# GpSimd keeps the gathers and the shuffles: the Wlin sum on VectorE, the value copy on ScalarE, gathers three to a step

## The reference

```python
embed_x = emb_table[X + offsets]             # [2048, 39, 64], a gather of rows of 256 bytes
att = embed_x
for i in range(3):                           # three layers, 2 heads of 32
    q, k, v = att @ WQ[i], att @ WK[i], att @ WV[i]
    attn = softmax(einsum('bihd,bjhd->bhij', q, k))
    att = relu(einsum('bhij,bjhd->bihd', attn, v) + att @ WR[i])
att_output = relu(att.reshape(B, 39 * 64) @ Wlin)
h = relu(embed_x.reshape(B, 39 * 64) @ W1 + b1)   # 512 wide
h = relu(h @ W2 + b2)                              # 256 wide
return sigmoid(att_output + relu(h @ W3 + b3))
```

## Time and profile before

| | before |
|---|---|
| median of three runs | 2331.08 us (2326.01 to 2338.38) |
| the profiled execution | 2338.26 us, span 2336.0 us, so 2.3 us lie around the span |
| TensorE | 2074.0 us busy, 89% of the span |
| VectorE | 1783.2 us, 76% |
| ScalarE | 1225.8 us, 52% |
| GpSimd | 1263.2 us, 54% |
| granted TensorE clock | 0.946 of full speed on the mean |

### The profile page before, as it was taken

One profiled execution on the slowest core, in us unless ns is written; L12 is line 12 of the kernel. 1 busy time (PEld: TensorE's weight loads), 2 busy tenths in 40 slices (PEclk: granted clock), 3 DMA queues, 4 the chain that ended last, 5 costly groups with the idle time before them and its releaser, 6 DMA issues. The chain is left out here.

```text
span 2336.0 us, 105692 instructions
## 1 busy us (share of the span) xinstructions
PE 2074.0 (89%) x44640; PEld 1687.1 (72%) x44640; DVE 1783.2 (76%) x3943; ACT 1225.8 (52%) x3397; POOL 1263.2 (54%) x1838
## 2 busy tenths in 40 slices
PE   1798998988989899898989989989898998989998
PEld 0577776867767777676777767778687776767887
DVE  2677786867868787786787868778687787878997
ACT  0455554645645455564555545556464555545665
POOL 6445555555555655556455555655656555565503
PEclk9999999989999999998999989999999999999998
DMA  4110011101101011010110101011010110101000
GB/s 137 26 26 24 24 28 24 28 22 24 28 23 28 23 28 25 23 29 21 27 26 25 28 22 28 23 25 29 22 30 23 27 25 24 29 21 27 23 20 15
DMA packets 67580, 64.76 MB, mean 28 GB/s; under 512 B 23768, under 2 KB 54504, under 8 KB 67112
## 3 DMA queue, kind: packets, MB, share of 16 engines
q1 hardware_dynamic: 47144, 37.52, 5.3%
q0 software_dynamic: 19968, 20.49, 4.6%
HBM read 27.24 MB, written 0.01 MB: 12 GB/s over the span
## 5 line engine op out<-in xcount | busy, mean ns | idle before, releaser
L314 POOL DMA_INDIRECT emb<-L_rec_emb_table,idx_t x624 | 640.1, 1026 | 532.5 <-PE Ob L472 350.2
L642 DVE TENSOR_REDUCE den<-pe_sb 103x16 f32<-103x624 f32 x384 | 308.5, 803 | 293.5 <-ACT pe_sb L567 277.6
L553 ACT ACTIVATE xs<-Ob 128x312 f32<-128x312 f32 x384 | 166.2, 433 | 672.1 <-PE Ob L472 661.8
L630 DVE TENSOR_REDUCE mx<-SV 103x8 f32<-103x312 f32 x768 | 365.1, 475 | 170.4 <-PE SV L455 156.4
L455 PE MATMUL SV<-yv,xs 64*39 64x142 f32 x12288 | 481.7, 296 | 10.7 <-ACT yv L560 8.0
L578 ACT COPY pt<-X 103x312 f32<-103x312 f32 x768 | 288.8, 423 | 259.3 <-PE X L441 201.3
L455 PEld LDWEIGHTS SV<-yv,xs 64*39 64x39 f32 x12288 | 359.3, 117 | 60.5 <-issue 10.4
L472 PEld LDWEIGHTS Ob<-pt,v_sb 39*32 39x32 f32 x12288 | 285.8, 109 | 152.7 <-issue 151.2
L472 PE MATMUL Ob<-pt,v_sb 39*32 39x39 f32 x12288 | 350.0, 201 | 51.5 <-ACT pt L578 25.9
L636 DVE TENSOR_TENSOR sd<-SV,mx 103x312 f32<-103x312 f32 x768 | 364.2, 474 | 0.0
L472 PE MATMUL Ob<-pt,v_x 39*32 39x39 f32 x12288 | 338.2, 202 | 25.7 <-issue 24.5
(11 more groups left out here) (74 smaller groups left out, 2670.5 us busy)
## 6 DMA issues: line engine op xcount, KB each, us to landing
v_x<-v_sb SPq DMA_DIRECT2D x768, 39.0 KB
emb<-L_rec_emb_table,idx_t POOLq DMA_INDIRECT x624
w<-L_rec_W SPq DMA_DIRECT2D x1, 4864.0 KB
w<-L_rec_W SPq DMA_DIRECT2D x1, 512.0 KB
idx_in<-r_X SPq DMA_DIRECT2D x1, 312.0 KB, 3.7
b_b<-L_rec_b SPq DMA_DIRECT2D x1, 256.0 KB
w<-L_rec_W SPq DMA_DIRECT2D x1, 128.0 KB
b_b<-L_rec_b SPq DMA_DIRECT2D x1, 128.0 KB
```

Of the source, the lines that this page charges most:

```text
L314: nc.gpsimd.indirect_dma_start(out=emb[:, n % ER, f % 2 * D:(f % 2 + 1) * D], out_offset=None, in_=table, in_offset=bass.IndirectOffsetOnA ...
L630: nc.vector.tensor_reduce(mx[:, gs, :], sv_scores[:, gs], AX.X, ALU.max).then_inc(mx_ready, 1)
L642: nc.vector.tensor_reduce(den[:], pe_sb[:], AX.X, ALU.add).then_inc(den_ready, 1)
```

## The change

It has four parts. `lin` leaves GpSimd: in steps whose unit is of the last layer ScalarE writes no relu; VectorE reads Ob with relu and the product with Wlin in one operation (`weighted`, tile `prod`) and sums it (`summed`). The values are copied by ScalarE in one operation behind the exponential, which is one operation over both halves now; the copy for the values of step s - 1 thus stands in ScalarE's step s, and scores of step s wait for it (`v_ready`) in place of `sd_ready`. `split_high` stands ahead of the copies of `yv`. The gathers come three to a step in 13 of the 24 steps and the shuffles at ts 8, 10, 12, 15 and 19, none of which has gathers; the gathers of a tile begin two steps earlier (`NEXT` 17, before 19). In tile 0 the first step has 10 gathers (before 9), then 2 in each of nine steps.

```diff
-    NEXT = 19
-    FIELDS_AT = [2, 1, 2, 1, 1, 2, 2, 2, 2, 1, 1, 1, 2, 2, 2, 2, 2, 1, 2, 2, 2, 1, 2, 1]
-    FIRST_FIELDS_AT = [9] + FIELDS_AT[5:6] * 8 + FIELDS_AT[9:18]
-    SHUFFLE_AT = {9: 0, 10: 1, 11: 2, 17: 3, 21: 4}
-    LIN_AT = {20: 0, 22: 1, 23: 2, 0: 3, 1: 4, 2: 5, 3: 6, 4: 7}
+    NEXT = 17
+    FIELDS_AT = [3, 0, 3, 0, 3, 0, 3, 3, 0, 3, 0, 3, 0, 3, 3, 0, 0, 3, 3, 0, 3, 0, 3, 0]
+    FIRST_FIELDS_AT = [10] + 9 * [2] + [1, 2, 1, 2, 2, 1, 2]
+    SHUFFLE_AT = {8: 0, 10: 1, 12: 2, 15: 3, 19: 4}
...
-    CHUNK_STEPS = chunk_steps(GATHERED, -LAG, 2 - LAG)
+    CHUNK_STEPS = chunk_steps(GATHERED, -LAG, -3)
...
     # TensorE
                 for j in range(2):
-                    at_least(pe, sd_ready, 2 * (u - 1) + j + 1)
+                    if j == 0:
+                        at_least(pe, v_ready, u)
...
-                at_least(pe, x_new, min(u, TOTAL))
+                if 0 < u <= TOTAL:
+                    if layer_of(u - 1) == L - 1:
+                        pe.wait_ge(lin_mult, last_outputs(u - 1))
+                    else:
+                        pe.wait_ge(x_new, outputs(u - 1))
...
     # ScalarE
-                if 0 <= u < TOTAL:
+                if 0 <= u < TOTAL and layer_of(u) < L - 1:
                     act.wait_ge(o_ps, u + 1)
...
                     nc.scalar.activation(xs[:, layer_of(u) + 1, layer_cols(u)], Ob[:, 0:C], ACTF.Relu).then_inc(x_new, 1)
                 if chunk_at(s - 1):
+                    at_least(act, o_ps, s - PV_AT)
                     evacuate_embedding(*chunk_at(s - 1))
+                if s + LEAD < TOTAL:
+                    split_high(s + LEAD)
...
                     at_least(act, pn_ready, u)
-                    for j in range(2):
-                        act.wait_ge(sd_ready, 2 * u + j + 1)
-                        nc.scalar.activation(half(pe_sb, j), half(sd, j), ACTF.Exp).then_inc(e_ready, 1)
-                if s + LEAD < TOTAL:
-                    split_high(s + LEAD)
+                    act.wait_ge(sd_ready, 2 * u + 2)
+                    nc.scalar.activation(pe_sb[:], sd[:], ACTF.Exp).then_inc(e_ready, 1)
+                    at_least(act, o_ps, u - VS + 1)
+                    nc.scalar.copy(v_sb[:, u % VS, :, :, :], sv_values).then_inc(v_ready, 1)
...
     # VectorE
+            def weighted(u):
+                dve.wait_ge(o_ps, u + 1)
+                if chunk_at(u + PV_AT):
+                    dve.wait_ge(embT_ready, chunk_count(*chunk_at(u + PV_AT)))
+                at_least(dve, lin_sum, last_outputs(u) - 1)
+                nc.vector.scalar_tensor_tensor(out=prod[:].rearrange("q (p f) -> q p f", f=F),
+                                               in0=Ob[:, 0:C].rearrange("q (p f) -> q p f", f=F), scalar=0.0,
+                                               in1=wl[:, None, :].to_broadcast([128, UP, F]),
+                                               op0=ALU.max, op1=ALU.mult).then_inc(lin_mult, 1)
+            def summed(u):
+                dve.wait_ge(lin_mult, last_outputs(u))
+                at = u // NU * NP + u % UL * UP
+                nc.vector.tensor_reduce(red[:, at:at + UP], prod[:].rearrange("q (p f) -> q p f", f=F),
+                                        AX.X, ALU.add).then_inc(lin_sum, 1)
...
                 for j in range(2):
...
-                    copied = nc.vector.tensor_copy(v_sb[:, s % VS, :, gs, :], sv_values[:, :, gs])
...
+                u = s - PV_AT
+                if u >= 0 and layer_of(u) == L - 1:
+                    weighted(u)
                 if s + LEAD < TOTAL:
                     split_low(s + LEAD)
+                if u >= 0 and layer_of(u) == L - 1:
+                    summed(u)
```

## The result

| | before | after |
|---|---|---|
| median | 2334.73 us (2326.01 to 2343.3) | 2211.76 us (2209.57 to 2213.95) |
| ratio | | 0.9473, interval 0.9433 to 0.9513 |
| span of the profiled execution | 2336.0 us | 2207.8 us |
| busy TensorE, VectorE, ScalarE, GpSimd | 2074.0, 1783.2, 1225.8, 1263.2 us | 2028.1, 1636.5, 1289.9, 887.0 us |

Faster, as forecast, but by 5.3% and not 12%: 2212 us lies outside the range (2015 to 2135). **First kind** of occasion is what this text calls the ones on which the kernel before took 2330 to 2335 us (the profile of before, the result and the first four experiments), **second kind** those on which it took 2297 to 2299 us (the other fourteen).

The account below looks back on a forecast made before the run. TensorE bounds undisturbed steps, GpSimd's lateness the steps around the `lin`s. Before, tile 0, tiles 1 to 14, tile 15 and end: 74.6 + 134 + 1720.6 + 112.5 + 17.3 = 2059.0 us of span, median 2055; range 2015 to 2135.

Parts of the forecast that it names:

- `lin` off GpSimd: Ahead of embedding transposes: the 102.2 us of waits for gathered rows go, and no stall takes their place.
- ScalarE and the new wait: In ScalarE's step: the value copy ends at +2.82, scores start at +3.18, so TensorE doesn't wait; 0 taken.
- rival C: ScalarE becomes the bound: scores wait 0.27 us for the value copy in 256 steps, 2125 us; chance 0.11.
- On VectorE: Per tile 19.9 us of value copies leave VectorE and 6.4 of sum come; worth 0.7 us, between 0 and 2.
- the clean tile: Tile 15's 113.4 us, plus step 0 at 5.8 and 20 embeddings at 0.1, less 0.7: 120.5 us.
- The stalls of ScalarE: ScalarE kept from its instructions while gathers run: one stall in two tiles, 1.4 us a tile, between 0 and 4.
- Three gathers in a step: Third gather ends at +3.87, attended starts at +4.28, so cost 0; only ts 17 collides, 1.0 us a tile.
- rival B: VectorE's normalization holds the third gather to +5.09, across attended: 0.6 us in 182 steps, 2164 us; chance 0.13.
- The measure to look for: Right: tiles 120 to 125 us, attended's unnamed idleness under 20, GpSimd under 900; rival B: third gathers 1.5 or more.

Follow-up runs that it names:

- the first four experiments: Two gathers a step 2049.43 us; bursts behind gather-free steps released by scores 2386.91; tiles 2 to 15 without gathers 2058.32; two a step, all released by scores 2923.21.
- kept awake: Changed kernel, GpSimd writing one column of zeros behind scores of each gather-free step that precedes a gather step: 2053.05 us, repeated 2056.56 and 2051.40.
- two-a-step list: Changed kernel's engines with gathers two to a step in 18 steps, three in ts 0: 2049.43 us on the first kind, 2034.73 on the second.
- the kernel with all gathers over attended: Two gathers a step, but every burst released by scores of the step before in place of attended: 2923.21 us, repeated 2144.00.
- the kernel with the burst brought forward: Changed kernel, but after a gather-free step GpSimd waits for scores of the step before in place of attended: 2386.91 us, ratio 1.0222.

## Why the prediction was right and wrong

*The span, term by term*, forecast against the result and against the same kernel on the second kind of occasion. Tiles 1 to 14 are what lies between the windows of tile 0 and tile 15.

| | forecast | result | second kind |
|---|---|---|---|
| before the first tile | 74.6 | 82.0 | 70.1 |
| tile 0 | 134 | 139.1 | 124.6 |
| tiles 1 to 14, each | 122.9 | 132.7 | 125.0 |
| tile 15 | 112.5 | 115.3 | 116.0 |
| end | 17.3 | 14.1 | 16.4 |
| span | 2059.0 | 2207.8 | 2077.7 |

*`lin` off GpSimd* was right: no embedding waits for gathered rows in the steady tiles, GpSimd is busy for 887 us (under 900), the shuffles fit, and the two engine moves alone give 0.9039 on an occasion of the second kind.

*ScalarE and the new wait* was right to 0.05 us (+2.77 for +2.82), and rival C, the wait of 0.27 us in 256 steps, isn't there. *On VectorE*: the clean tile was set too low, 120.5 against a measured floor of 122.0 to 122.4 on the first kind of occasion, so 21 to 27 us over 14 tiles. The 0.7 us a tile of relief, the sum of both moves, was not measured by itself. What is measured is that without the copy's move the time is 45 us longer, some 2.1 us in each of 14 tiles and the rest in the first and the last, so the copy's move is what lets VectorE take the sum.

*The stalls of ScalarE*, 1.4 us a tile, didn't come: relu begins 0.04 us after attended's last matmul in the step shown. They belong to gathers that start just at attended's end, and these bursts start 0.27 us behind it or later. So the term should have been nothing: two relus of 256 began over 0.3 us late.

*Three gathers in a step* is the step that failed. "The third starts at +2.93" took the first gather's +0.35 from the earlier trace rows, a step behind one with gathers. The kernel before gathers in every step, so its trace had no first gather behind a gather-free step; there it starts at +0.84, as it does in 10 of the 13 bursts (+0.97 and +1.01 in steps 17 and 20), after 7 us of idleness or after 2. And it took all gathers at a pitch of 1.25 to 1.29 us, where a first gather at +0.84 is itself held by `split_low` and costs 0.2 us more. The prediction had the third gather begin 0.53 us ahead of the normalization and clear attended by 0.4 us. In 7 of the 13 bursts it begins some 0.1 us or more behind the normalization's start, is held, and lies over the whole of attended until +5.09; in 3 more it ends where attended begins. The number +5.09 is the one that rival B gave for a held gather. So B happened, though not for its own reason, a gather held when the normalization begins 0.53 us into it: as the forecast assumed, a gather that begins ahead of the normalization isn't held, be it 0.63 us ahead (kept awake) or 0.02 (the step 2 shown above).

The second thing taken without a row was that a gather which clears attended costs nothing. On the second kind of occasion that is so. On the first kind even the bursts of steps 7 and 14, whose third gather starts at +2.84, earlier than forecast, and ends 0.5 us before attended, lost 0.3 us each; the gather of the earlier trace rows, which ended half a microsecond ahead of attended in the kernel before, had shown no loss.

The Trainium skill, *SBUF — State Buffer*, section *SBUF: two separate sides*, says that VectorE and GpSimd share a pair of ports, that a VectorE operation with two SBUF inputs takes it against a GpSimd operation that reads SBUF, and that whichever starts first has it for the whole instruction while the other blocks. A gather reads its row numbers from `idx_t` in SBUF. The trace agrees for a gather that begins under the normalization (1.54 us, ending 0.82 behind it). It disagrees when the gather is first: with a gather already begun, 0.02 to 0.63 us before, the normalization still took 0.81 to 0.84 us.

*The price* of a collision, which rival B put at 0.6 us, is 1.1 in the step shown on the first kind (6.12 for 5.01) and 0.4 on the second. In all, third gathers cost 10.7 us a tile over the two-a-step list (132.7 against 122.0, 150 us) on the first kind, and 2.6 (125.0 against 122.4, 37 us) on the second. With the late start known, and the middle of the 0 to 2.2 us of the earlier trace rows, the forecast would have been 2055 + 1.1 x 10 x 14 = 2209. That it comes so near 2212 is luck: 1.1 is the price on one kind of occasion, only 7 of the 10 steps hold a gather, and the clean tile is still 1.5 us too low. On the second kind the kernel took 2077, inside the stated range, with the same failed step in it, at 37 us.

*The measure to look for* worked: of what the prediction named as signs of B, third gathers of 1.5 us and attended stretched in gather steps, both are in the profile; the unnamed idleness of attended was 78.8 us where under 20 was to be right.

What stays open is what makes an occasion of the first kind. It isn't the chip as such, for one chip met both. The kernels and their data are the same, and their packets took as long: those of the gathers' queue 4.7% of 16 engines' 2207.8 us for the changed kernel on the first kind, 5.1% of 2077.7 on the second; the 357 instruction fetches 1.1 and 1.2%. The first kind shows in three places: the kernel before at 2330 us or more, 74.6 to 87.1 us ahead of the first tile in place of 69.1 to 71.4, and no time from issue to landing in the profile's last part, where the second kind has 2.5 to 2.7 us for the gathers and 9 to 17 us for the loads of the weights. So something differed in how the executions were run or recorded; the record doesn't say what. In the opening burst of the two-a-step kernel TensorE all but stops on the first kind, and runs through on the second. From 70 to 80 us, first kind:

```profile
70.00:80.00 10.00, 1.68 (x8) 0.88 (x7) 0.48 (x1) 0.00 (x0) 6.34 (x7) 0.76 0.13 26
```

Second kind:

```profile
70.00:80.00 10.00, 9.15 (x161) 7.05 (x161) 8.95 (x20) 5.57 (x15) 7.49 (x8) 1.00 0.18 42
```

That the engines' instructions come to them more slowly while GpSimd works on a gather would fit; it was not tested.

## What to carry to other kernels

A place in a step that is clear by less than half a microsecond isn't clear: read what the engine did in the step before, since GpSimd's first gather behind a gather-free step came 0.5 us later than behind a gather step, and look for every two-operand VectorE operation that a gather can start under, since it then ends 0.8 us behind that operation and pushes those after it. Spread gathers so that none lies over a stretch of many small matmuls, ends just as it starts, or starts at its end: two a step were worth 42 us over three on an occasion of the second kind and 162 on the first, and this list (0.8789 and 0.8847 of before) beats both kernels on either. Repeat the kernel under study beside the experiments that explain it, before believing them: the changed kernel's third gathers cost four times as much on one occasion as on another, and the kernel with all gathers over attended lost eight times as much.

## What of the hardware was not expected

- GpSimd's first gather behind a step without a gather started 0.77 us after attended's end, with 7 us of idleness ahead of it and also with 1.8 to 2.8 us behind a shuffle; it was 0.27 us where the step before had a gather or GpSimd had written one column (98 ns) behind scores.
- A gather (0.94 us) that starts under a normalization ends 0.82 us after it: so 96 of 107 in the changed kernel's trace, the others having started in its first 0.04 us or behind 0.7. Of 80 that began 0 to 0.65 us ahead of it none was held. Under `split_low`, the other operation with two SBUF operands, it is the same, and there some that began 0.1 to 0.35 us ahead were held too.
- Gathers started within 0.1 us of attended's end kept ScalarE from an instruction whose operands were there, for 0.7 to 4.5 us on the first kind of occasion (66 of 68 such steps of the kernel with the burst brought forward) and 0.3 to 0.9 us on the second (77 of 78, two a step over attended). Where they started 0.2 to 0.4 us behind it, ScalarE began 0.05 us after attended's end (mean of 159 steps of the kernel with the engine moves alone).
- The same kernel with all gathers over attended took 2923 us on one occasion and 2144 on another, clock 0.90 and 1.00 in its steady tiles, while the two-a-step kernel, with none there, took 2049 and 2035.
